# Loads of raw weights: issued by ACT ahead of a cell's evacuation, or by SP between the moves

## The reference

```python
def _cell(w, bias, ins):
    x = jnp.concatenate(ins, axis=1)              # 1 to 3 streams of 16 channels
    y = lax.conv_general_dilated(x, w, window_strides=(1, 1), padding='SAME', ...)
    y = jax.nn.relu(y + bias[None, :, None, None])
    right, up, down = jnp.split(y, 3, axis=1)
...
x = x + _L0_conv_ref(_gn(x), L0_conv_W, L0_conv_b)
x = x + _L1_conv_ref(_gn(x), L1_conv_K)
x = x + _L2_conv_ref(_gn(x))
x = x + _L3_conv_ref(_gn(x), L3_conv_W, L3_conv_b)
```

## Time and profile before

| | |
|---|---|
| median of 3 runs | 434.03 us (434.0 to 434.24) |
| the profiled execution | 435.94 us, span 434.1 us |
| TensorE busy | 403.1 us, 93% |
| DVE busy | 301.6 us, 69% |
| ACT busy | 199.4 us, 46% |
| POOL busy | 205.2 us, 47% |
| DMA queue of SP | 30.8% of the 16 DMA engines' span |
| DMA queue of POOL | 23.4% |
| granted TensorE clock | 0.98 of full speed |

### The profile page before, as it was taken

The page is one execution under the profiler, slowest core; times in us unless marked ns, Lnnn a source line. Parts: engine busy times, 40 slices in busy tenths (PEclk is TensorE's granted clock), DMA queues, the critical chain, the costliest instruction groups (busy, mean ns, idle before and its releaser), DMA issues.

```text
span 434.1 us, 12447 instructions
## 1 busy us (share of the span) xinstructions
PE 403.1 (93%) x5149; PEld 202.5 (47%) x5149; DVE 301.6 (69%) x563; ACT 199.4 (46%) x307; POOL 205.2 (47%) x384
## 2 busy tenths in 40 slices
PE   8999998989999897985998899999999999997884
PEld 5444444445554444543444455445444554444442
DVE  5789967537975346679587789968645954539684
ACT  7555533545526336465201455533545325347363
POOL 6277657955647433300000267657965594442300
PEclk9999999999999998999798999999999999998999
DMA  6076587868879665520000066588677797551701
GB/s 230 13 248 139 130 189 200 190 129 191 186 148 172 130 143 95 122 43 2 1 2 2 12 175 144 127 201 194 155 152 153 142 182 138 98 98 39 111 2 50
DMA packets 27304, 52.90 MB, mean 122 GB/s; under 512 B 11632, under 2 KB 13296, under 8 KB 27248
## 3 DMA queue, kind: packets, MB, share of 16 engines
q1 hardware_dynamic: 14416, 30.24, 30.8%
q0 software_dynamic: 12544, 21.14, 23.4%
q10 hardware_dynamic: 288, 0.72, 0.4%
HBM read 12.81 MB, written 0.52 MB: 31 GB/s over the span
## 4 chain that ended last, share of the span: by engine, by line
PE 57%; POOL 14%; DMA 11%; DVE 8%; ACT 5%; issue 3%; SPq 0%; DVEq 0%; ACTq 0%
PE bank L554 38%; PE bank L598 18%; POOL inp L534 11%; DMA inp<-cell_out 10%; POOL shifts L524 3%; ACT act_out L787 2%; DVE cell_out L1006 2%; DVE inp L718 1%; DVE inp L973 1%; DMA raw<-weights_in 1%; ACT cell_out L781 1%; ACT inp L718 1%; DVE inp L725 1%; DVE stat L860 1%; PE bank L617 1%
## 5 line engine op out<-in xcount | busy, mean ns | idle before, releaser
L534 POOL DMA_DIRECT2D inp<-cell_out x320 | 169.0, 536 | 142.1 <-DVE cell_out L1006 139.1
L787 ACT ACTIVATE act_out<-bank,bias 128x512 f32<-128x512 f32 x160 | 105.3, 687 | 101.3 <-PE bank L598 58.0
L554 PE MATMUL bank<-inp,w_heavy 128*32 128x512 f16 (+1 forms) x1536 | 139.8, 384 | 4.9 <-DMA inp<-cell_out 2.5
L1006 DVE TENSOR_TENSOR cell_out<-act_out,cell_out 128x512 f16<-128x512 f32 x156 | 107.8, 695 | 51.0 <-ACT act_out L787 47.0
L554 PE MATMUL bank<-inp,w_light 96*32 96x512 f16 (+2 forms) x1440 | 119.4, 395 | 12.8 <-DVE inp L973 10.3
L554 PEld LDWEIGHTS bank<-inp,w_heavy 128*32 128x32 f16 (+1 forms) x1536 | 65.1, 102 | 71.0 <-issue 13.8
L554 PEld LDWEIGHTS bank<-inp,w_light 96*32 96x32 f16 (+2 forms) x1440 | 59.8, 104 | 70.7 <-issue 19.8
L781 ACT ACTIVATE cell_out<-bank,bias 128x512 f16<-128x512 f32 x56 | 38.9, 694 | 87.0 <-PE bank L554 64.6
L598 PE MATMUL bank<-cell_out,w_first 32*128 32x512 f16 x1296 | 72.1, 378 | 0.0
L524 POOL DMA_DIRECT2D shifts<-inp x48 | 29.6, 623 | 59.0 <-DMA inp<-cell_out 58.8
L1000 DVE CAST cell_out<-act_out 128x512 f16<-128x512 f32 x100 | 42.9, 429 | 14.2 <-ACT act_out L787 13.5
(11 more groups left out here) (53 smaller groups left out, 170.1 us busy)
## 6 DMA issues: line engine op xcount, KB each, us to landing
inp<-cell_out SPq DMA_DIRECT2D x96, 72.2 KB, 3.6
inp<-cell_out SPq DMA_DIRECT2D x96, 71.2 KB, 3.8
raw<-weights_in SPq DMA_DIRECT2D x8, 672.0 KB, 5.0
inp<-cell_out POOLq DMA_DIRECT2D x128, 36.1 KB, 3.0
raw<-weights_in SPq DMA_DIRECT2D x8, 576.0 KB, 5.0
inp<-cell_out POOLq DMA_DIRECT2D x128, 35.1 KB, 3.2
shifts<-inp POOLq DMA_DIRECT2D x16, 144.5 KB, 3.1
inp<-cell_out POOLq DMA_DIRECT2D x32, 72.2 KB, 4.4
```

The lines of the kernel that those rows point to most:

```text
L534: pool.dma_start(to, source).then_inc(signal, 16)
L554: last = pe.matmul(bank[j % BANKS][p:p + m, :], home[i][0:rows, w:w + m], source[:, off:off + PAIRS, dx:dx + SIDE], start=n == 0, stop=n = ...
L787: act.activation(act_out[:, n % T_RING, :], bank[j % BANKS][:, :], ACT.Relu, bias=bias[:, col + part[k]:col + part[k] + 1], scale=1.0 / W_ ...
L1006: dve.tensor_tensor(low, t, high, ALU.subtract).then_inc(cell_written, 1)
```

## The change

The loop over `cells` in SP's program loses the loads of raw weights and keeps the moves. The two loads at SP's start stay. ACT's program gets a function `load_weights(st)`, called at the head of its `grid_cell`, ahead of `evacuate(st)`. It issues the same loads at the same place in the order of cells, each after the same wait for `weights_ready`, now on ACT. For the first cell of the second grid's half 0, which ACT evacuates outside `grid_cell`, it is not called; no load is due there.

```diff
@@ SP
-                if p >= RAW_RING:
-                    sp.wait_ge(weights_ready, p - RAW_RING + 1)
                 sp.dma_start(raw[0:rows, p % RAW_RING, 0:width], weights[i, 0:rows, 0:width]).then_inc(
                     raw_loaded[p % RAW_RING], 16)
...
-            ahead = RAW_RING
-            for at, st in enumerate(cells):
-                while at and ahead < len(splits) and split_no[splits[ahead - RAW_RING]] <= 2 + len(
-                        [i for o in cells[:at] for i in AFTER.get(o[1:], [])]):
-                    load_weights(ahead)
-                    ahead += 1
+            for st in cells:
                 bank_no = -1
@@ ACT
+            def load_weights(st):
+
+                at = cells.index(st)
+                split = 2 + len([i for o in cells[:at] for i in AFTER.get(o[1:], [])])
+                while loaded[0] < len(splits) and loaded[0] - RAW_RING < split and at:
+                    p = loaded[0]
+                    i = splits[p]
+                    rows, blocks, _ = WEIGHTS[scheme_of(SETS[i])]
+                    width = blocks * width_of(SETS[i])
+                    act.wait_ge(weights_ready, p - RAW_RING + 1)
+                    act.dma_start(raw[0:rows, p % RAW_RING, 0:width], weights[i, 0:rows, 0:width]).then_inc(
+                        raw_loaded[p % RAW_RING], 16)
+                    loaded[0] += 1
+
+            loaded = [RAW_RING]
+
             def grid_cell(st):
+                load_weights(st)
                 evacuate(st)
                 for i in AFTER.get(st[1:], []):
                     weights_high(i)
```

## The result

The changed kernel took **446.5 us** (median of 4 runs, 443.86 to 448.51) against 434.01 us (433.86 to 434.24) for the kernel before. The ratio is 1.0284 (95% interval 1.0229 to 1.0338): 12.5 us slower, where the prediction said 3.4 us, with 440.9 as its upper end. The profiled execution took 446.08 us, 10.1 more than that of before, so its trace holds most of the difference.

A forecast was written before the change was run, and what follows sets the result against it. TensorE, busy 93% of the span, sets the pace, with other chains running level. First grid 1.0 us (0.2 left after column 2, 0.8 in column 3) plus second grid 2.4 makes 3.4 us: 437.4 us, range 434.4 to 440.9.

The forecast's parts named there:

- Column 0: First cells of each grid: DVE idles 1.42 us per late first cast, putting TensorE 3.15 us behind, then 2.4.
- Rival 2: Column 0 and column 3: each issue on ACT takes 1.0 us instead of 0.58; about 440 us; chance 0.09.
- The relief for `down`: First grid, columns 1 and 2: without loads ahead in SP's queue, `down` moves land in 3.6 to 5 us.
- Rival 1: No relief for `down`: ACT's loads hold up SP's moves as before; total 4.8 us, 438.8 us; chance 0.18.
- The give-back: First grid after column 0: shorter waits for `down` shrink TensorE's lag from 3.15 to 0.2 us by (2,2).
- cost of these: nothing: Loads in columns 1 to 3: ACT catches up within the cell, so they cost nothing; without cover, about 0.6 us each.
- about level: Second grid, (1,1) and (1,2): `down` moves land about level with the delayed TensorE, costing 0.5 us more or nothing.
- Column 3: First grid, (3,0) of half 0: 0.20 us of wait and 0.63 of issue on the path, 0.8 us.
- the old stalls of 0.73 and 1.19: First grid, (2,1) and (2,2) of half 0: TensorE starts level with before, then 0.2 us late.

The follow-up runs named there:

- wait_only: The kernel before, SP's loads as they were, with only the waits for weights_ready put on ACT ahead of the evacuation: 437.32 us, 1.0079.
- before_again: Control: the kernel before, unchanged, run against itself under another name on the same chip: 433.2 us, 1.0039.
- after_again: The changed kernel once more, on a second chip, against the kernel before: 444.98 us, 1.0282.
- three_back: The changed kernel with all waits on ACT, but three of thirty loads (p 12, 26, 27) back on SP: 445.96 us, 1.0331 against the kernel before.
- act_three: The kernel before with only three loads (p 12, 26, 27) on ACT, with their waits: 440.43 us, 1.0185.
- wait_rest: The kernel before, all loads on SP, with waits and an 8-column DMA issue on ACT at the twenty places outside column 0: 436.77 us, 1.0085.
- act_col0: The kernel before with only the ten column-0 loads on ACT, the other twenty on SP: 439.02 us, 1.0138.
- wait_issue: The kernel before, loads still on SP, with ACT's waits and an 8-column DMA into a spare tile behind each: 440.13 us, 1.0173.
- load_behind: The changed kernel with each ACT load and its wait behind the cell's evacuation instead of ahead: 437.26 us, 1.0132 against the kernel before.
- ring4: The changed kernel with four raw-weight buffers, which made ACT load one set earlier behind the same waits: 441.53 us, 1.0242 against the kernel before.
- ring4_nowait: The changed kernel with four raw-weight buffers, same loads at the same places, ACT's waits already met: 437.02 us, 1.0052 against the kernel before.
- tiny_after: The changed kernel with loads from the fourth on cut to 8 columns (output differs): 434.99 us, 1.0073 against the kernel before.
- tiny_before: The kernel before with loads from the fourth on cut to 8 columns (output differs): 430.67 us, 0.9963.
- act_rest: The kernel before with the twenty loads outside column 0 on ACT with their waits, the ten of column 0 on SP: 445.66 us, 1.0265.

## Why the prediction was wrong

The sign was right, and so was the mechanism in column 0. The sum was 3.4 us and the measured difference 12.5, more than three times as much. By its own steps:

**Column 0: right, its term too large.** DVE's timeline of the kernel after: the first and the last of the four late first casts (the two between, at 30.54 and 37.46, idled 1.29 too), and the copies of both grids:

```profile
24.62 0.43 DVE L1010 CAST cell_out<-act_out 128x512 f16<-128x512 f32 x1 [1.29 <-ACT act_out L780]
...
44.94 0.43 DVE L1010 CAST cell_out<-act_out 128x512 f16<-128x512 f32 x1 [1.27 <-ACT act_out L780]
...
51.92 1.36 DVE L983 COPY inp<-inp 64x2176 f16<-64x2176 f16 x2
...
284.81 1.35 DVE L983 COPY inp<-inp 64x2176 f16<-64x2176 f16 x2
```

Less the starts in the earlier trace rows, DVE is 1.33, 1.36, 2.33 and 3.69 late, where 1.50, 1.66, 2.76 and 4.26 were predicted, and the copies are 3.71 late. The chain is ACT's, and reads so in ACT's timeline:

```profile
23.37 0.34 ACTq L795 DMA_DIRECT2D raw<-weights_in  x1
23.81 2.42 ACT L780 ACTIVATE act_out<-bank,bias 128x512 f32<-128x512 f32 x4 [3.85 <-DVE w_first L863]
```

Four evacuations in 2.42, as in the earlier trace rows; in front of them a wait for DVE's low part and an issue of 0.34 us. The size that was off is the issue: 0.58 was taken from SP, while on ACT all 30 took the same:

```profile
L795 ACTq DMA_DIRECT2D raw<-weights_in x30: 334/335/357, 16.6 to 371.5; - x30
```

The gaps between the steps were larger, 0.25 us in all and not 0.15. So the idle DVE is 1.29 and not 1.42, and TensorE was 2.60 behind instead of 3.15 in the first grid, and 1.6 instead of 2.4 in the second (6.97 less 5.36). The waits for DVE's low part that carry it are new. The waits of the kernel after have six such groups; the largest (us, times, longest):

```profile
ACT act_out L780 <- DVE w_heavy L863: 26.5, 6, 6.0
```

Most of their time (87.2 us in the six) cost nothing, since ACT would have waited for TensorE. `wait_only` measures what they do cost by themselves: 0.8%. Rival 2, a slow issue on ACT, is refuted by the 0.34 us.

**The relief for `down`: the step that failed first.** The forecast had the moves land in 3.6 to 5 us once no load stands ahead of them in SP's queue. Time to landing of SP's moves of 61.8 to 63.8 in the kernel after, and of those of 294.7 to 297.1:

```profile
DMA to landing us min/median/max: 3.6/4.0/6.4
...
DMA to landing us min/median/max: 4.5/4.9/6.5
```

The median fell from 6.9 to 4.0, but TensorE waits for the last: 7.2 became 6.4. Issued up to 63.7 instead of 60.0, it landed at 70.1, and the stall ahead of (1,1) was 1.52 instead of 1.31 long. What counts is the load's bytes, not its queue: 2.8 to 3.1 us with loads of 8 columns. **Rival 1 came nearest** here, to which the prediction gave 0.18: it had 2.75 and 1.9 us pass through to (1,1) and (1,2), and 2.90 and 2.64 were measured. That the first of these agrees so well is partly luck: the last move was issued 3.7 us later than before and landed 0.8 faster, where the rival had 2.75 and no change. What the prediction overweighted was the comparison of the earlier trace rows with the earlier trace rows: there the load was not only ahead in the queue but alive at the same time, and the earlier trace rows had a POOL move, on another queue, at 6.80 us in the same stretch. The Trainium skill ("DMA: Bandwidth & Descriptors", "Issuing engines are not separate DMA queues") says the same, that DMAs share the engines whoever issues them and that another issuer saves only the time of issue; the landings of 6.4 and 6.5 us agree.

**The give-back, and "cost of these: nothing": the steps that failed most.** The forecast let TensorE wait less for `down` (4.83 us before) and put nothing at the loads of columns 1 to 3. The sums of TensorE's stalls ahead of columns 1 and 2, from the timelines, which I take for waits for `down` as the prediction did (the page puts some down to ACT or to nothing):

| kernel | first grid | second grid |
|---|---|---|
| before | 4.83 | 0 |
| `before_again` | 2.79 | 0 |
| after | 6.05 | 2.04 |
| `after_again` | 5.70 | 1.98 |
| `three_back` | 5.63 | 1.34 |
| `act_three` | 4.47 | 0.19 |
| `wait_rest` | 4.54 | 0 |
| `act_col0` | 1.98 | 2.36 |
| `wait_issue` | 1.79 | 3.48 |
| `load_behind` | 3.73 | 2.23 |
| `ring4` | 3.40 | 0.90 |
| `ring4_nowait` (its longest execution) | 7.01 | 0 |
| `tiny_after`, `tiny_before` | 0 | 0 |

One profile each, so a difference of 2 us in a line proves little; but the change, whole or less three loads, stands at 7.0 to 8.1 us in all, the two profiles of before at 4.8 and 2.8, and no such stall is left where the loads carry no bytes. That bytes make the landings long is shown by this. That ACT's waits, by making the issue of the moves late, are the other half is supported by the time of `ring4_nowait`, but not by its one profile, of its longest execution, which has as long waits as the change. The second grid shows it best, where `down` was to be "about level". The moves of (1,0) of half 0 took 6.5 us to land, as before (6.7), and were issued 9.3 to 9.5 us later than before (the first at 294.8 against 285.3), some 2.4 more than TensorE's 7.0; nearly all of the 2.04 us of stall is that. The forecast had set aside 0.5 at most.

Had it gone by rival 1 throughout, the sum would have come nearer. `after_again`, counted from its own stall at 42.37 (1.12 later than in the kernel after), is 3.1, 2.7 and 3.3 us behind the earlier trace rows at (1,1), (1,2) and (2,2) of half 0: the lag passes through, as rival 1 has it. With 0.8 for column 3, and in the second grid 1.6 for column 0 and 2.1 for the stall behind it, that is 7.8 us. It is also all by which this execution outlasts the profiled one of before (443.0 less 434.1, less the 1.12): what the clock took and gave in it cancels out. In the kernel after it does not, as follows. Of the 12.5 us between the medians, the two profiles hold 10.1.

At single cells the order of issue comes in as well. SP's program had kept each load behind the moves that were due before it, which the prediction did not see; on ACT that order is gone. Chain of the kernel after, in order of time:

```profile
63.71 6.42 DMA inp<-cell_out
...
94.48 8.53 DMA inp<-cell_out
```

The second is the `down` move that a load issued 0.6 us earlier went with, and TensorE stood for 2.95 us. `act_three` has this stall too with three loads moved; `act_rest` against `wait_rest` puts 1.8% on the later loads beyond their waits and issues.

**What follows a stall.** The clock was not in the sum: 2.8 and 1.6 us behind the two new stalls, 2.0 back between the grids. The price of a stall was taken to be its length. The kernel before pays this price too, between the grids and, in `before_again`, behind a stall of 2.79 us (2.77 us for twelve matmuls), so not all of it can be put down to the change.

**Column 3: right.** 0.8 was predicted for (3,0); the stall grew from 2.50 to 3.32, and the lag from 6.53 at (2,2) to 7.36. That at (2,1) and (2,2) the old stalls of 0.73 and 1.19 would go was right too (nothing and 0.25 are left), but by luck: TensorE came 7 us later.

The lag of 10.8 us at 312 us in this one pair of profiles is thus 2.6 + 1.6 for column 0, 0.8 for column 3, 2.95 and 2.0 for the two new stalls, 4.4 for the clock behind them, and what the clock gave back between the grids, 2.0; these make 12.4, of which 1.7 was taken up by stalls of before that went, and 10.7 is left. At the end of the span it is 10.2.

**What stays open.** `three_back` had none of the three loads on ACT and was as slow as the change; the other 27 were there, and all the waits. How much of the loss at the later cells comes from single loads that pass a move, and how much from landing times that are spread wider over the whole kernel, the runs do not tell. Nor is it shown why `ring4_nowait`, with the same loads on ACT, lost so little: ACT is not held up by DVE there, so moves can be issued earlier, but its only trace is of an execution as slow as the change. And the long executions of `act_three` have no trace. The parts need not add up, so no share is given for each.

## What to carry to other kernels

A DMA that is moved to another engine's queue takes its bytes along and leaves its order behind: the neighbours in time still pay for it, and whatever the old queue kept ahead of it may now be overtaken. In this kernel the waits and the moved loads cost more together than either alone. Before a semaphore wait goes into a compute engine's queue, list what stands behind it, and get the wait met beforehand (a fourth buffer: 1.0052 instead of 1.0282; by the medians 1.1% instead of 2.8) rather than moving the work. Where several chains run level with the bound, the places at which a stall is absent deserve the same sum as those at which one is seen.

## What the hardware showed beyond what was expected

An issue on ACT took 334 to 357 ns in all 30 cases of the kernel after, against 333 to 1435 ns for 24 of these loads on SP; once the wait had ended, 0.44 us passed from the start of the issue to the first evacuation (23.37 to 23.81).

Moves of 71 or 72 KB between parts of SBUF landed in 2.8 to 3.1 us beside loads of 8 columns (`tiny_after`), in up to 6.4 and 8.5 (after) and 8.1 us (`act_three`) beside a load of 576 or 672 KB issued by ACT, and in up to 7.2 us beside one issued by SP.

The clock fell from 2.4 towards 1.2 GHz behind idle stretches of TensorE in some places and not in others. Behind stalls of 2.95 and 2.04 us (after), 2.86 (`act_three`) and 1.98 (`act_col0`) twelve matmuls took 2.77, 2.77, 2.04 and 2.00 us instead of 1.51. Behind 3.18 us (`load_behind`) they took 1.62, behind 2.20 in `wait_rest` and 1.98 in the second grid of `after_again` they took 1.51. Nor did the 2.50 and 3.32 us ahead of (3,0) show in the 17.84 us of the matmuls behind them. In these traces a stall of 2 to 3 us cost up to as much again (2.8 us behind 2.95), and its length alone does not tell whether it will.
